# Last tokens normalised in the projection stage, keys and queries loaded first in attention, and the last pair of groups without unused work

## What is computed

```python
xn = _layernorm(x, axis=-1)                       # eps 1e-5
s  = attention(xn, wq, wk, wv, wo)                # 32 heads of 32, 8 key/value heads, rope, causal
# the feed-forward branch, on xn
x_norm  = layer_norm(xn, in_gamma, in_beta)       # eps 1e-6
thought = x_norm[:, -1, :] @ agg_w + agg_b        # the last token of each sequence only
for _ in range(4):
    t = layer_norm(thought, pn_gamma, pn_beta)
    t = gelu(t @ d1_w + d1_b)                     # 1024 -> 4096
    thought = thought + (t @ d2_w + d2_b)         # 4096 -> 1024
broadcast = (thought @ bc_w + bc_b)[:, None, :]
gate = sigmoid(xn @ gate_w + gate_b)
g = silu(layer_norm(xn + gate * broadcast, out_gamma, out_beta))
out = x + s * g
```

## Time and profile before

| | us |
|---|---|
| median of 3 runs | 2773.43 (2772.71 to 2775.95) |
| profiled execution, device time | 2770.51 |
| its span (first to last instruction) | 2768.4 |
| projection | 0 to 600.2 |
| attention: prelude | 600.2 to 648.0 |
| attention: 32 turns | 648.0 to 2010.6 |
| attention: behind the turns | 2010.6 to 2029.8 |
| output | 2030.1 to 2768.4 |

### The profile page before, as it was taken

The page is one execution under the profiler, slowest core; times in us unless marked ns, Lnnn a source line. Parts: engine busy times, 40 slices in busy tenths (PEclk is TensorE's granted clock), DMA queues, the critical chain, the costliest instruction groups (busy, mean ns, idle before and its releaser), DMA issues. The chain is left out here.

```text
span 2768.4 us, 45646 instructions
## 1 busy us (share of the span) xinstructions
PE 2584.0 (93%) x14400; PEld 1717.1 (62%) x14400; DVE 1759.4 (64%) x3577; ACT 1032.5 (37%) x1650; POOL 1369.4 (49%) x627
## 2 busy tenths in 40 slices
PE   5999999979999999999999999999959999999998
PEld 4888888864444444444444444444438888888886
DVE  6444444446666666667666676666747777777777
ACT  2111111104555555555555555555531111111111
POOL 1111111125898878888788887889821111111111
PEclk9999999988999999999999999999979999999999
DMA  6444444445644645545456454464566555666556
GB/s 243 174 171 171 171 171 174 160 151 183 193 147 153 192 126 176 166 149 180 129 174 190 127 179 154 147 192 149 160 199 124 114 114 115 124 132 121 114 114 121
DMA packets 228288, 432.05 MB, mean 156 GB/s; under 512 B 16472, under 2 KB 98520, under 8 KB 228176
## 3 DMA queue, kind: packets, MB, share of 16 engines
q1 hardware_dynamic: 154784, 378.74, 41.6%
q0 software_dynamic: 73392, 51.91, 12.6%
HBM read 316.56 MB, written 113.51 MB: 155 GB/s over the span
## 5 line engine op out<-in xcount | busy, mean ns | idle before, releaser
L882 DVE CUSTOM_DVE_ANT_0 bcast<-mxp,mask_q 128x128 f32<-128x128 f32 (+7 forms) x1054 | 754.0, 754 | 422.7 <-PE mxp L998 274.2
L799 ACT ACTIVATE pr<-stp 128x512 f32<-128x512 f32 x1152 | 667.1, 598 | 557.6 <-PE stp L1007 313.5
L1007 PE MATMUL stp<-qs,ks 97*128 97x512 f32 x1152 | 504.0, 451 | 31.1 <-ACT pr L799 24.5
L426 PE MATMUL eo<-xt,w 128*128 128x512 f32 x1920 | 449.3, 393 | 3.6 <-DVE xt L369 3.6
L750 POOL TENSOR_TENSOR acc<-acc,pr 128x2048 f32<-128x2048 f32 x96 | 439.1, 4574 | 14.2 <-ACT pr L799 9.8
L426 PEld LDWEIGHTS eo<-xt,w 128*128 128x128 f32 x1920 | 359.2, 189 | 77.5 <-issue 4.0
L1007 PEld LDWEIGHTS stp<-qs,ks 97*128 97x128 f32 x1152 | 211.5, 188 | 315.1 <-ACT pr L799 157.7
L1370 PE MATMUL gp<-g,xa 128*128 128x512 f32 x1536 | 355.9, 391 | 17.1 <-DMA xa<-xt_scratch 17.1
L1370 PE MATMUL op<-o,ya 128*128 128x512 f32 x1536 | 355.6, 391 | 10.9 <-DVE ya L1313 10.9
L1370 PEld LDWEIGHTS gp<-g,xa 128*128 128x128 f32 x1536 | 290.0, 189 | 78.4 <-DMA xa<-xt_scratch 17.9
L1370 PEld LDWEIGHTS op<-o,ya 128*128 128x128 f32 x1536 | 289.8, 189 | 71.7 <-DVE ya L1313 11.3
(11 more groups left out here) (139 smaller groups left out, 2878.8 us busy)
## 6 DMA issues: line engine op xcount, KB each, us to landing
wch<-in_d_w SPq DMA_DIRECT2D x132, 1024.0 KB, 10.1
qs<-q_scratch SPq DMA_DIRECT2D x201, 256.0 KB, 7.3
xa<-xt_scratch POOLq DMA_DIRECT2D x66, 512.0 KB, 6.1
xt_scratch<-xt SPq DMA_DIRECT2D x16, 2048.0 KB, 14.4
q_scratch<-r SPq DMA_DIRECT2D x64, 512.0 KB, 3.2
yr<-y_scratch POOLq DMA_DIRECT2D x33, 512.0 KB, 5.8
xs<-in_x SPq DMA_DIRECT2D x33, 512.0 KB, 5.5
y_scratch<-ys SPq DMA_DIRECT2D x65, 256.0 KB, 2.0
```

The costliest lines, as they stand in the source:

```text
L426: last = nc.tensor.matmul(out, lhs[a](k), rhs[c](k), start=(k == 0 and (a, c) == (0, 0)), stop=(k == KT - 1 and (a, c) == (1, 0)))
L799: nc.scalar.activation(pr[half][:, :, at:at + P], stp[u % 2][:].rearrange("p (h t) -> p h t", h=REP), ACT.Exp, scale=SCALE).then_inc(act_d ...
L882: last = nc.vector.tensor_tensor_reduce(out=bcast[:, k % 2, hh * step:hh * step + w], in0=mxp[k % 2][:, hh * step:hh * step + w], in1=mask ...
L1007: last = nc.tensor.matmul(bank, ks[par][:, j * P:(j + 1) * P], qs[par][:, :, i * P:(i + 1) * P], start=True, stop=i != j)
```

## The change

1. The last tokens are normalised in the projection's last half: three loads after its `xt` store, VectorE's ten small instructions after rope of q = 1 (with GpSimd's two powers there), eight transposes on TensorE after q = 3's product, and a copy to the new tile `xlt`. The attention's prelude only copies `xlt` into `t_in`.
2. The prelude's loads begin with keys and queries; the weights `agg_w` come next and the small vectors and `v` behind them. The fill of `pr` goes from VectorE to GpSimd, `x_last()` goes.
3. The last step is written out behind a loop of three steps, with its own copy of the loop over c. Its last two turns get a number `left`: where it is 2 or 1, what would be loaded or computed for a group that doesn't exist is left out: the loads, the 20 pieces `mx 0` to `mx 19`, `mt 0` and its move, and the layer norm behind the last step. In the last turn the product with `bc_w` is put into the plan (`ga`, `gc` after unit 23, `gb`, `gs` after unit 31), from `th` directly.

```diff
@@ PLAN_TEXT
-23: mx 12
+23: mx 12, ga, gc
...
-31: mx 18
+31: mx 18, gb, gs
@@ project_phase, SyncE
+                    if final and half:
+                        sp.wait_ge(tr_done, KT * NB)
+                        sp.dma_start(xl, x.rearrange("(b t) d -> b t d", b=B)[:, T - 1, :]).then_inc(xl_in, 16)
+                        for dst, v in ((gl, in_g), (bl, in_b)):
+                            sp.dma_start(dst, v.partition_broadcast(B)).then_inc(gb_in, 16)
@@ project_phase, GpSimd
+                        if final and half and q == 1:
+                            for k in range(2):
+                                pool.wait_ge(l_ve, k + 1)
+                                nc.gpsimd.tensor_tensor(lrs, lve, mhalf[0:B, 0:1], ALU.pow).then_inc(l_rs, 1)
@@ project_phase, VectorE
+                dve.wait_ge(xl_in, 16)
+                for k, eps in enumerate((EPS_X, EPS_F)):
+                    for c in range(2):
+                        last = nc.vector.bn_stats(lst[:, c, :], xl[:, c * 512:(c + 1) * 512])
+                    link(last)
+                    link(nc.vector.bn_aggr(lmv, lst.rearrange("p a b -> p (a b)")))
+                    nc.vector.tensor_scalar(lve, lmv[:, 1:2], eps, None, ALU.add).then_inc(l_ve, 1)
+                    dve.wait_ge(l_rs, k + 1)
+                    link(nc.vector.tensor_scalar(xl, xl, lmv[:, 0:1], lrs, ALU.subtract, ALU.mult))
+                dve.wait_ge(gb_in, 32)
+                link(nc.vector.tensor_tensor(xl, xl, gl, ALU.mult))
+                nc.vector.tensor_tensor(xl, xl, bl, ALU.add).then_inc(xl_done, 1)
@@ project_phase, TensorE
+                        if q == 3 and final and half:
+                            pe.wait_ge(xl_done, 1)
+                            for k in range(KT):
+                                last = nc.tensor.transpose(tr[0][:, k * B:(k + 1) * B], xl[:, k * P:(k + 1) * P], ident[0:B, 0:B])
+                            last.then_inc(xlt_full, 1)
@@ attention_phase
         def turns(engine, turn):
-            with engine.Fori(0, STEPS) as s:
+            with engine.Fori(0, STEPS - 1) as s:
                 with engine.Fori(0, CH - 1) as c:
                     for par in range(2):
                         turn(s, c, par, uses[0])
                 for par in range(2):
                     turn(s, CH - 1, par, uses[par])
+            with engine.Fori(0, CH - 1) as c:
+                for par in range(2):
+                    turn(STEPS - 1, c, par, uses[0])
+            for par in range(2):
+                turn(STEPS - 1, CH - 1, par, uses[2 * par], 2 - par)
@@ SyncE, prelude
-            sp.dma_start(xl, xlast).then_inc(xl_in, 16)
-            for r in range(B):
-                sp.dma_start(gl[r:r + 1, :], in_g).then_inc(gb_in, 16)
-                sp.dma_start(bl[r:r + 1, :], in_b).then_inc(gb_in, 16)
             load_k(0, 0)
             load_q(0, 0, 0)
             load_q(1, 0, 0)
-            load_v(0, 0)
+            load_w(0, whole(agg_w))
+            load_w(1, whole(agg_w))
...
+            load_v(0, 0)
@@ GpSimd, prelude
+            nc.gpsimd.memset(pr[1][:, :, PROB_W[1] - 768:], 1.0).then_inc(init_p, 1)
@@ TensorE, turn
+                            if ahead and left == 1:
+                                continue
...
+                        elif e[0] == "ga" and "ga" in use:
+                            pe.wait_ge(t_done, STEPS + 2)
+                            burst(0, tb + use["ga"], th32, (GROUPS + 2) * 32)
+                        elif e[0] == "gb" and "gb" in use:
+                            burst(1, tb + use["gb"], th32, (GROUPS + 2) * 32)
@@ TensorE, behind the turns
             values(1, 7, 1)
-            pe.wait_ge(t_done, STEPS + 3)
-            burst(0, LAST, h_in, (GROUPS + 2) * 32)
-            burst(1, LAST + 1, h_in, (GROUPS + 2) * 32)
             pe.wait_ge(add_done, NADD * GROUPS + 4)
-            prob_sums(1, LAST + 2)
+            prob_sums(1, LAST)
```

More of the change, by code:

```diff
@@ L646, in _, with turn @@
             load_q(0, 1, 0)
-            def turn(s, c, par, use):
+            def turn(s, c, par, use, left=3):
                 it = s * CH + c
@@ L978, in _ @@
             turns(dve, turn)
[L979 to L983 removed]
+            reciprocals(1, GROUPS, LAST)
         @block.tensor
```

169 lines of the change are left out of this document (79 added, 90 removed).

## The result

The changed kernel took 2758.57 us in the median of six executions (2756.35 to 2758.70), the kernel before, beside it, 2773.80 (2772.31 to 2781.73): 15.2 us less, a ratio of 0.994 with an interval of 0.993 to 0.995. In a second row of runs it was 2760.06 against 2774.37, a ratio of 0.9948 (0.9935 to 0.9962), 14.3 us. The forecast was 2758.2. That the number is right says less than it seems to. The two profiled executions, 2770.51 and 2758.57 us, are only 11.9 apart, and of the three terms of the sum the third (the end) held, the first (the start of attention) was a little too large and the second (the last step) clearly.

What follows compares the result with a forecast made beforehand. The page's chain of waits was followed to TensorE's matmuls in the output stage, which shifts as a block; GpSimd's additions bound the last turn. 5.0 + 3.9 + 6.3 = 15.2 us off 2773.4 gave 2758.2, range 2754.0 to 2764.5.

Steps and rivals of the forecast that it cites:

- the end: Last turn, bounded by GpSimd's additions: final sums start 8.3 us earlier, 2.0 lost to the low clock, net 6.3 us.
- the start of attention: Attention's prelude: keys and queries land earlier and VectorE's maxima start sooner, 5.7 us less 0.7 for the transposes, 5.0.
- the last step: Boundary ahead of turn 24: without the jump to the step's start, its code fetch is saved, 3.9 us.
- Transposes: Projection, between the matmuls of q = 3 and q = 4: eight uncovered transposes on TensorE cost 0.7 us.
- Rival C: Prelude: `agg_w` lands late, so it gains only 2.05 us instead of 5.0; 2761.2 us, chance 0.07.
- Rival A: Turn 24: running on costs as much as the jump, or the 3.9 us had another cause; 2762.1 us, chance 0.14.
- B: Last step's copied loop: its jumps at turns 26 and 28 stall, up to 7.8 us; say 2762 us, chance 0.09.
- D: Last step: code in sequence isn't ahead of the engines, each of eight turns pays 3.9 us; 2793.3 us, chance 0.03.
- the sums of group 30: Last turn on TensorE: without pieces `mx 0` to `mx 7` they come at 1982.7 for 1984.40, 1.7 us sooner.
- the clock cost: End of attention: TensorE, idle before, starts at 1.2 GHz; sums lose 0.9 us and the spreading 1.1, together 2.0.

Runs made afterwards that it cites:

- the run with late bursts: The changed kernel with the last pair's two `bc_w` bursts put back behind the last turn's products, before the row sums; 2759.70 us, ratio 0.996 to the kernel before.

## Why the prediction was right, and where it was not

**Transposes: right.** They took 0.66 us (573.01, eight on TensorE), and the projection's last half from q = 0 to the start of the values grew from 54.43 to 55.26 us, 0.8 for the 0.7. VectorE was through with the last tokens at 565.7 and TensorE waited for nothing, as worked out. The row:

```profile
573.01 0.66 PE L493 MATMUL tr<-ident,xin 4*128 4x4 f32 x8
```

**Start of attention: right in kind, too large by 0.6.** Net 5.3 us in the first pair of profiles. Over all, turn 1's load comes at 685.8 with the new start (mean of 11 profiles, 684.6 to 687.2) and at 690.2 with the old (mean of 3): 4.4 for the 5.0 forecast. The step that failed is "the first queries land as much earlier, since the queue was empty before". Behind the first key load TensorE starts after 7.96 to 8.16 us in the three profiles with the old start and after 7.95 to 9.44 in the eleven with the new one, 0.7 us later in the mean. The weights queued behind the queries are not the reason that the runs show, as said above; why the queries land later, and why so unevenly, stays open. Rival C, the late weights, was not seen.

**The last step written out: the mechanism right, the size wrong.** The failed step is "The turn behind the jump to the step's start costs 45.67 - 41.76 = 3.9 us more". Both rows were read rightly, but the first turn is one at a granted clock of 0.96 and the second at 1.00, and half-clock stretches come at the boundary without the jump as well. The written-out step is worth 3.0 us here, of which the jump is some 2.7 (2.6 in the pair of turns 23 and 24 of the run that changed only this). The prediction's own view of stretches, used for the prelude, would have shown the clock. Rival A is out in its first half, since running on costs nothing, and true in its second for a part: 1.2 of the 3.9 us were the clock. B and D are out, the copies' turns are ordinary ones. Of 18 turns that run on into a new step 16 took 41.4 to 42.4 us; the two others are those that waited for `t_in`. The changed kernel's own turn 24 is at the upper end of these, 42.1 to 42.4 us in five profiles, and its turn 25 some 0.4 us shorter than others; why was not asked. The Trainium skill, Runtime: NRT & Kernel Launch, section Instruction fetch mechanics, says the same of both, without a price: a taken branch to code further off waits for a fetch, code that follows is fetched ahead. The runs agree, with 2.7 us for a jump and 41.73 us for the turn that runs on into a new step.

**The end: right.** 6.1 us for 6.3 in the first pair of profiles, 5.7 between the means (107.5 of the four that were alike, 101.8 of five; with the fifth of the old ones, 111.03, it would be 6.4). Its terms: the sums of group 30 came 1.8 us earlier against turn 30 (forecast 1.7), GpSimd bound the turn, the last sums took 1.94 us (forecast the same), the spreading 8.45 (forecast 8.2), so the clock cost 2.2 us for 2.0. TensorE's idle time was 7.5 us and not 10, which changed nothing: the run with late bursts shows that even 4.6 bring the sums down to 1.93.

**The sum.** With the sizes found, 4.4 + 3.0 + 5.7 = 13.1 us where 15.2 was forecast. The medians gave 15.2 and 14.3, with intervals from 13.9 to 19.4 and from 10.5 to 18.0. Executions of one kernel differ by 2 to 15 us in these rows of runs, in part with the number of half-clock stretches, so that none can tell 13.1 from 15.2. That the forecast of 2758.2 met the median within 0.4 us was luck: by its terms it should have been some 2 us off.

## What to carry to other kernels

Before a slow turn is priced by its neighbour, compare the granted clock of both stretches: a part of the difference may be a clock stretch that comes back elsewhere when its cause is gone. Price an end by what idles beside it: here work that stood behind the last wait fitted into 7.5 us of idle time ahead of it, for 4.8 us and nothing else. And where the code has room, try writing loops out, outer and inner: by the account that was worth 15.8 us here (1220.2 - 1204.4), about as much as all that the change did.

## What the chip showed that was not expected

- TensorE's clock falls inside dense turns as well. In the changed kernel's turn 9 it stood at 1.2 GHz for some 3.4 us; TensorE had been 39% busy in one of the microseconds ahead of it, where it waited 0.61 us for a maximum of VectorE, and 90% or more in the others. The rows of those microseconds (PEclk is the third number from the end):

```profile
1053.00:1054.00 1.00, 0.39 (x2) 0.30 (x2) 1.00 (x3) 0.60 (x1) 1.00 (x1) 1.00 0.14 55
...
1055.00:1056.00 1.00, 0.90 (x5) 0.47 (x4) 1.00 (x3) 0.71 (x2) 1.00 (x1) 0.87 0.00 0
1056.00:1057.00 1.00, 1.00 (x4) 0.44 (x3) 0.68 (x3) 0.06 (x1) 1.00 (x1) 0.50 0.02 8
...
1059.00:1060.00 1.00, 1.00 (x10) 0.35 (x3) 0.00 (x0) 0.00 (x0) 1.00 (x1) 0.93 0.00 0
```

  All stretches away from the boundaries begin at the same place of their turn, 30 to 31 us in, but most turns, with the same work and the same wait, have none. What decides between them stays open.
- At the step boundaries there are one to three such stretches, with the jump (2.2 on average over 24 boundaries) and without it (1.8 over 18).
- Writing out the 24 turns inside the loops over c took 0.38 us off each, 8.8 us over turns 1 to 29, with 31 more instruction packets on one queue and no wait for code that the turns' lengths show.
- VectorE's additions and products of 128x32 elements, 0.19 us each, took 2.0 to 3.5 us where they met one of GpSimd's additions, and ended 0.04 us behind it. In the same stretch VectorE's maxima of 128x1024 out of `mxp` kept their 1.21 to 1.23 us beside GpSimd's work.
